# A two-layer audio tower on one core: step 0's state sum through TensorE and ScalarE, and a later load of M3

## What is computed

```python
h = tok(x, W1, b1, W2, b2)                              # patches of 16, two layers
h = h + attn(layernorm(h), w_q, w_k, w_v, w_o)          # quantised, 16 heads
h = h + expert(layernorm(h), w_gate, w_expert, b)       # top-1 of 8, capacity 100
h = h + ssm(layernorm(h), phazor...)                    # a complex decay along the sequence, real part
h = h + moe(layernorm(h), Wg, W1, W2, W3)               # top-2 of 8 experts, 256 -> 512 -> 256
```

## Time and profile before

| what | value |
| --- | --- |
| median of 3 runs | 494.39 us (494.08 to 496.92) |
| profiled execution | 493.69 us, span of its instructions 492.0 us |
| mean granted TensorE clock | 0.951 |
| TensorE matmul busy | 424.3 us (86%) |
| TensorE weight load busy | 263.0 us (53%) |
| VectorE busy | 288.3 us (59%) |
| ScalarE busy | 200.4 us (41%) |
| GpSimd busy | 170.5 us (35%) |
| DRAM traffic | 76 GB/s over the span |

### The profile page before, as it was taken

One profiled execution on the slowest core, in us unless ns is written; L12 is line 12 of the kernel. 1 busy time (PEld: TensorE's weight loads), 2 busy tenths in 40 slices (PEclk: granted clock), 3 DMA queues, 4 the chain that ended last, 5 costly groups with the idle time before them and its releaser, 6 DMA issues.

```text
span 492.0 us, 9443 instructions
## 1 busy us (share of the span) xinstructions
PE 424.3 (86%) x3489; PEld 263.0 (53%) x3490; DVE 288.3 (59%) x885; ACT 200.4 (41%) x373; POOL 170.5 (35%) x141
## 2 busy tenths in 40 slices
PE   0889999995887874878989999999999999999991
PEld 0645456453564653745656766666654444456651
DVE  0498779686688999999996488527751111111110
ACT  1224744662577433325534653255322232333330
POOL 6042010110010115642154536453254565556322
PEclk9999999998887976899899999999999999999996
DMA  9999410046037100563012422152132222322221
GB/s 166 254 202 200 88 48 4 14 156 220 8 94 291 31 20 1 175 223 117 11 45 48 102 39 48 24 137 45 19 57 33 44 37 44 47 45 43 45 23 21
DMA packets 35468, 40.22 MB, mean 82 GB/s; under 512 B 5216, under 2 KB 30048, under 8 KB 35296
## 3 DMA queue, kind: packets, MB, share of 16 engines
q1 hardware_dynamic: 26192, 29.91, 23.0%
q0 software_dynamic: 7040, 9.44, 12.0%
q10 hardware_dynamic: 2192, 0.27, 0.6%
HBM read 28.47 MB, written 8.91 MB: 76 GB/s over the span
## 4 chain that ended last, share of the span: by engine, by line
PE 56%; DVE 18%; DMA 10%; issue 6%; ACT 5%; SPq 3%; POOLq 0%; POOL 0%; DVEq 0%; ACTq 0%
PE psum L2371 21%; PE psum L2392 11%; PE psum L1967 9%; DMA M3s<-in_x_dram 4%; PE psum L1981 3%; DMA out_dram<-O,dst_i 3%; PE psum L2381 3%; DMA out_dram<-O,dst_high 2%; PE psum L1993 2%; PE psum L2353 1%; DVE st_att L1063 1%; SPq L340 1%; DVE H L1313 1%; PE psum L2011 1%; DVE Eb L1105 1%
## 5 line engine op out<-in xcount | busy, mean ns | idle before, releaser
L1860 DVE TENSOR_TENSOR QT<-QT,psum 128x512 f32<-128x512 f32 x36 | 24.7, 687 | 116.0 <-PE psum L2371 113.9
L2371 PE MATMUL psum<-M1s,KT 128*128 (+2 forms) x176 | 68.9, 601 | 2.0 <-issue 1.5
L2392 PE MATMUL psum<-M3s,KT 128*128 (+1 forms) x352 | 69.3, 383 | 1.3 <-ACT KT L855 0.8
L2371 PE MATMUL psum<-M2s,KT 128*128 (+2 forms) x176 | 67.7, 592 | 0.0
L2392 PEld LDWEIGHTS psum<-M3s,KT 128*128 128x128 f32 (+1 forms) x352 | 50.2, 170 | 24.5 <-issue 16.6
L1967 PE MATMUL psum<-M2s,M1s 128*128 128x512 f32 x128 | 58.9, 604 | 0.7 <-ACT H L720 0.7
L866 ACT ACTIVATE O<-psum,gate_slot 128x256 f32<-128x256 f32 x36 | 17.1, 475 | 100.3 <-PE psum L2392 97.4
L522 POOL DMA_INDIRECT KT<-mixture_rows_in,src_i x36 | 40.6, 1127 | 32.3 <-issue 18.0
L2371 PEld LDWEIGHTS psum<-M2s,KT 128*128 128x128 f32 (+1 forms) x176 | 26.0, 171 | 35.8 <-issue 35.8
L549 POOL DMA_INDIRECT out_dram<-O,src_i x17 | 31.4, 1849 | 33.9 <-ACT O L866 14.1
L851 ACT ACTIVATE QT<-psum 128x512 f32<-128x512 f32 x36 | 21.5, 597 | 40.2 <-PE psum L2371 40.2
(11 more groups left out here) (444 smaller groups left out, 786.6 us busy)
## 6 DMA issues: line engine op xcount, KB each, us to landing
M3s<-in_x_dram SPq DMA_DIRECT2D x4, 1024.0 KB, 13.5
M3s<-in_L_ffn_W_dram SPq DMA_DIRECT2D x1, 4096.0 KB, 15.7
M2s<-in_L_ffn_W_dram SPq DMA_DIRECT2D x1, 4096.0 KB, 15.3
M1s<-in_L_ffn_W_dram SPq DMA_DIRECT2D x1, 4096.0 KB, 14.5
M3s<-in_x_dram SPq DMA_DIRECT2D x4, 992.0 KB, 16.8
M1s<-vtok SPq DMA_DIRECT2D x64, 34.0 KB, 1.9
out_dram<-H SPq DMA_DIRECT2D x4, 512.0 KB, 4.1
M1s<-in_L_tok_W_dram SPq DMA_DIRECT2D x2, 512.0 KB, 14.6
```

The lines of the kernel that those rows point to most:

```text
L1860: v.tensor_tensor(sil[:, u, :], sil[:, u, :], bank[3], ALU.mult).then_inc(v_gated, 1)
L2371: last = mm(z[rows, :], xrT[:, u, c, rows], w[:, e, c, :].rearrange("p a h -> p (a h)"), start=(c == 0), stop=(c == CH - 1))
L2392: last = mm(bank[6][rows, 0:DM], actT[:, u, c, rows], M3s[:, e, c, :].rearrange("p a d -> p (a d)"), start=(c == 0), stop=(c == HC - 1))
```

## The change

TensorE no longer only turns step 0's state rows. `state_added` puts H into PSUM first, by a matmul of each H tile with the identity, and accumulates the turned state rows onto it, again by matmuls with the identity. VectorE takes step 0's statistics from PSUM and no longer writes H; it then gives `v_ssm_added` and asks GpSimd by a second small instruction. ScalarE copies the sum from PSUM to H (`ssm_rows`, signal `a_ssm_rows`) and goes on. The rows of H to the output (step 0) and `state_rows(1)`, which uses the same banks, wait for that copy. For steps 1 to 3 the sum stays as it was.

`NORM2_ACT` becomes 1, so ScalarE also writes step 1's normalised rows after the attention. M3's load moves from behind step 1's V transfers to behind step 3's.

```diff
-        NORM2_ACT = 2
+        NORM2_ACT = 1
@@ SP
-                if i == 1:
+                if i == 2:
+                    sp.wait_ge(p_layer1, CH * STEPS)
+                    sp.dma_start(M2s[:], M2.rearrange("e (c p) h -> p e c h", p=P)).then_inc(d_moe, 16)
+                if i == 3:
                     sp.wait_ge(a_sorted, STEPS - 1)
                     sp.wait_ge(v_plane, (STRIDE - RH) * STEPS)
                     sp.dma_start(M3s[:], M3.rearrange("e (c p) d -> p e c d", p=P)).then_inc(d_m3, 16)
-                if i == 2:
-                    sp.wait_ge(p_layer1, CH * STEPS)
-                    sp.dma_start(M2s[:], M2.rearrange("e (c p) h -> p e c h", p=P)).then_inc(d_moe, 16)
...
-                sp.wait_ge(v_ssm_added, i + 1)
+                if i < 1:
+                    sp.wait_ge(a_ssm_rows, i + 1)
+                else:
+                    sp.wait_ge(v_ssm_added, i + 1)
@@ ScalarE
+            def ssm_rows(i):
+
+                act.wait_ge(v_ssm_added, i + 1)
+                a.activation(H[:, TS * i:TS * (i + 1), :].rearrange("p t d -> p (t d)"), banks(4), ACT.Copy
+                             ).then_inc(a_ssm_rows, 1)
+
+            ssm_rows(0)
             gate_exp(2)
             act.wait_ge(v_probsT, BT * STEPS)
+            act.wait_ge(a_ssm_rows, 1)
             norm(SR, 0, X4[0], v_norm4_in, a_norm4)
@@ VectorE
                 dve.wait_ge(p_ssm_rows, i + 1)
+                if i < 1:
+                    norm_stats(S, lambda t_: bank[4 + t_ // 2][:, DM * (t_ % 2):DM * (t_ % 2 + 1)])
+                    v.tensor_scalar(S["ve"][:], S["mv"][:, :, 1], EPS, None, ALU.add).then_inc(v_ssm_added, 1)
+                    dve.wait_ge(v_ssm_added, i + 1)
+                    ask(v.tensor_scalar(S["ve"][:], S["ve"][:], 1.0, None, ALU.mult))
+                    return
@@ TensorE
+            def state_added(i, z):
+
+                def rows(t):
+                    return z[t // 2][:, DM * (t % 2):DM * (t % 2 + 1)]
+
+                for k in range(2):
+                    for t in (k, k + 2):
+                        mm(rows(t), ident[:], H[:, TS * i + t, :], start=True, stop=False)
+                    if k == 0:
+                        pe.wait_ge(v_ssm_out, i + 1)
+                    for t in (k, k + 2):
+                        for c in range(CH):
+                            last = mm(rows(t)[:, P * c:P * (c + 1)], uR[i % 2][:, SN * c + P * t:SN * c + P * (t + 1)],
+                                      ident[:], start=False, stop=(c == CH - 1))
+                last.then_inc(p_ssm_rows, 1)
...
             pe.wait_ge(v_att_rows, STEPS)
-            state_rows(0, bank[4:6])
+            pe.wait_ge(v_ffn_added, 1)
+            state_added(0, bank[4:6])
...
-            pe.wait_ge(v_ssm_added, 1)
+            pe.wait_ge(a_ssm_rows, 1)
             state_rows(1, bank[4:6])
```

More of the change, by code:

```diff
@@ L298, in audio_tower_kernel @@
             sem(n) for n in "a_slot_out a_embed a_expert a_k_masked a_part".split())
-        a_sorted, v_biases, a_plane, v_plane = (
-            sem(n) for n in "a_sorted v_biases a_plane v_plane".split())
+        a_sorted, v_biases, a_plane, v_plane, a_ssm_rows = (
+            sem(n) for n in "a_sorted v_biases a_plane v_plane a_ssm_rows".split())
         block = ctx.enter_context(nc.Block())
```

## The result

| what | before | after |
| --- | --- | --- |
| median | 495.65 us (4 runs, 494.08 to 496.94) | 489.94 us (4 runs, 487.96 to 490.32) |
| profiled execution | 493.69 us, span 492.0 | 489.62 us, span 487.9 |
| mean granted TensorE clock | 0.951 | 0.954 |

The ratio is 0.9878, with a 95% interval from 0.9831 to 0.9925: 1.2% faster, and the interval reaches to within 1% of before. The forecast, 487.6 us against a median of 494.39, was a ratio of 0.9863, with a range of 485.2 to 491.0.

What follows compares the result with a forecast made beforehand. Bound by VectorE from 144 to 251 us and TensorE in the expert slots from 251 to 480, with a TensorE stop in values(1). 3.35 + 2.4 + 0.7 + 0.35 = 6.8 us off 494.39 gave 487.6, range 485.2 to 491.0.

Steps and rivals of the forecast that it cites:

- The stop: TensorE's issue wait in values(1), laid to M3's load delaying an instruction packet: 4.35 us falls to 1.0, gaining 3.35.
- the last term: In values(1), the 1.6 us from the packet's end to TensorE's resumption; if it was load too, no stop is left.
- The clock: Step 3's first three layer-2 tiles, slow after the stop, return to 0.87 us each: 2.4 us gained, other end 0.
- M3's new place: M3's load behind step 3's V transfers costs nothing; other end 2.3 us if the first packet met its traffic.
- NORM2_ACT: Step 1's normalised rows move from VectorE to ScalarE: 0.7 us gained at att_mean(2), ends 0 and 1.2.
- The state sum: Step 0's state sum on TensorE instead of VectorE: 0.35 us gained at state_sum(1), ends -0.3 and 1.1.
- from 207.62 this ends at 211.1: TensorE's matmuls for step 0's state sum take 3.46 us; VectorE wants them at 210.93 and waits 0.2 to 0.3.
- (3): Rival: TensorE runs state_added and what follows at half clock, 7.5 us lost against 6.45 won, 495.4 us; chance 0.02.
- The hold: GpSimd's product holds the port pair shared with VectorE, delaying small operations before state_sum(1); without it 0.55 us gained.
- the likeliest case: The forecast with its own ends, 485.2 to 491.0 us for the whole kernel; chance 0.75.
- (1): Rival: M3's load isn't the cause, the stop in values(1) stays at 4.35 us, time 493.3 us; chance 0.13.
- (2): Rival: the stop moves to step 3's scores under M3's traffic, 492.3 us at worst; chance 0.07.

Runs made afterwards that it cites:

- e4: The changed kernel with 32 instead of 52 warm-up matmuls at TensorE's start; median 487.36 us, ratio 0.9829.
- e9: The changed kernel with three empty instructions on VectorE behind sort_x(0); median 489.26 us, ratio 0.9890.
- e13: e12 with six filler matmuls while TensorE stands idle ahead of the second half of values(3); median 487.47 us, ratio 0.9825.
- e11: e12 with state_added(0) issued ahead of the last three expert tiles of step 2; median 488.63 us, ratio 0.9871.
- e1: The kernel before with only M3's load moved behind step 3's V transfers; median 491.05 us, ratio 0.9892.
- e2: The changed kernel with M3's load put back behind step 1's V transfers; median 494.84 us, ratio 0.9977.
- e5: The kernel before with M3's load at its old place in the queue, but also waiting for the end of step 1's values; median 489.13 us, ratio 0.9885.
- e12: The changed kernel with 32 instead of 52 warm-up matmuls and three empty instructions on VectorE; median 488.36 us, ratio 0.9841.
- e6: The kernel before with 32 instead of 52 warm-up matmuls, M3's load where it was; median 489.74 us, ratio 0.9896.
- e10: e12 with step 0's state sum back on VectorE as in the kernel before; median 487.49 us, ratio 0.9843.

## Why the prediction was right

**The stop.** Right in its mechanism, 0.6 us off in size. I took 1.0 us as what would be left and 1.8 as the end; 1.63 was left, and 1.36 to 1.63 in the six kernels with the load away and nothing shifted. My own terms gave 0.6 + 1.1 + 1.6 - 1.9 = 1.4, and after's are 1.0 + 1.2 + 1.5 - 2.1 = 1.6. So 0.4 of the 0.6 us come from going below that sum in case the last term was load; it wasn't, since 1.3 to 1.5 us from the packet's end to the resumption were there in all six. The start of the packet, which I sized at 0.6 us after the block's entry and which took 1.0 to 1.4, was too small, and the loop (2.10 by the earlier trace rows, not 1.9) makes up for half of it. Gain 2.72 us instead of 3.35.

**The clock.** 2.01 + 1.71 + 1.27 - 1.06 - 0.86 - 0.87 = 2.20 us came back, of 2.4 forecast. The 0.2 between them is no clock: the first tile takes 1.06 us, and not 0.87, in e4 too, which has no stop. A stop of 1.4 to 1.6 us did not lower the clock in any of the six.

**M3's new place.** Right that it costs nothing, though by the slack and not by the packets' good timing: one did meet the traffic (3.9 us), in a stretch with room for it. Step 3's scores and values have no stop. M2's load held a packet back by 4.4 us in before's own trace; I had not counted that block, and it would have spoken for the mechanism.

**NORM2_ACT.** 0.73 us at `att_mean(2)`, forecast 0.7 (0.9 to 1.0 in the other nine kernels that have it). Not foreseen: the 0.46 us idle that the shorter program of VectorE brought with it, of which 0.34 stayed.

**The state sum.** Wrong in sign in the profiled execution: -0.36 us instead of +0.35 (it was +0.5 in e4, e9 and e13). The operations cost about what I priced (3.7 us on TensorE, 1.42 for the statistics from PSUM, 1.03 for ScalarE's copy). The step that failed is "from 207.62 this ends at 211.1": it took the start from before's row, where the eight transposes ahead of it had been at full clock. I had weighed the slow clock as a rival for `state_added` itself (3), and there it did not come; it came one piece of work earlier, where 0.8 us are enough to turn this part. The bound from below (-0.3) was nearly its value. The hold by which a small copy took 0.85 us is there again in e11 (0.66 us, until GpSimd's product ends), as the Trainium skill ("SBUF — State Buffer", two separate sides) has it; but `state_sum(1)` follows 0.14 us behind the product, so the hold costs none of the 0.54.

**The sum.** 2.72 + 2.20 + 0.73 - 0.34 - 0.36, and some 0.24 between the rows, make the 5.19 us by which the slots open earlier. Forecast were 6.8. The median fell by 5.7 us (4.5 against the 494.39 of the forecast, whose fourth run came later), and the time lies inside the range: two terms were too large, one had the wrong sign and one cost was not foreseen, 1.6 us in all, and the likeliest case came about. Of its signs, the stop under 2 us, the tiles at 0.87 and, but for 0.2 us, `state_added` in 3.5 us were met. The transposes came 5.0 us earlier and not 6, and VectorE's 1.26 us before step 0's statistics, where under 0.5 was to show it right, is the state sum's failure. VectorE idle for over 0.5 us before `att_mean(2)` was a bad sign: before had 0.54 already, and after has 0.77.

**The rivals.** (1), that M3's load isn't the cause, falls by e1, e2 and e5, though its weaker half stands: the block comes 1.4 to 1.6 us too late without the load as well. The rule of the Trainium skill ("Runtime: NRT & Kernel Launch", instruction fetch mechanics), that crossing a block's boundary is mostly hidden, holds at the other boundaries that I counted through, `values(0)` in e11 to e13 (below) excepted. It fails where 127 small matmuls with their weight loads run through a block in 2.1 us: 1.63 us quiet, 4.35 with a load. (2), a stop in step 3, did not come. (3) came in a smaller form.

## What to carry to other kernels

A stop with "issue" as its only cause in the middle of a loop of tiny matmuls was a missing block of instructions here: look for the packet, and then either keep large transfers away from it or shift the program (by 40 instructions here), so that the block runs out among large ones. Either gave 1% here, and the kernel that has both, with the change's other two parts (e4), 1.7%. A shift moves all the boundaries behind it, so look at the other loops too: `values(0)` below. And when work moves onto an engine whose clock changes, price the work ahead of it at the slow clock too: the new work's start, not its length, turned this part from a gain into a loss.

## What I had not expected of the hardware

A stop can appear in an earlier loop without any load. In e11, e12 and e13, all with 32 warm-up matmuls, `values(0)` stops for 1.07 to 1.12 us, and in e4, e6 and e10, with the same start of the program, it doesn't. The chain of waits of e12, and the packet in the 0.2 us from 83.2:

```profile
82.58 2.01 PE psum L2030 x118
84.59 1.12 issue
85.71 0.32 PE psum L2030 x5
```

```profile
q8 instruction: 1, 0.02, 33.2%
```

In e4 and e10 there is a packet in the 0.2 us from 78.0 and from 77.2, and the next at 85.2; in e12 none between 72.4 and 83.2. TensorE's work is the same in all of them up to there. So a packet can come 5 us late with nearly no traffic, and I have no cause for it. The same holds for one of before (from 124.4, 3.7 us after its block's entry at 120.9) and one of after (from 126.6, entered at 118.3, with no transfers at all between), which stopped nothing. The reverse stands too: M1's load did not delay the packet at 210.30, and no run here says why.

The clock differs between executions of nearly the same work: `norm2_columns(2)` took 1.09, 1.20, 1.53, 1.64, 1.87, 1.88 and 1.97 us in the profiles. And in e1 two of the first layer-2 tiles, at 35.9 us, ran at the slow level (2.07 and 1.27 us, against 1.13 and 0.86 in after), which put e1's whole profile 1.45 us behind. That, the slots' spread of 1.6 us and the stop in `values(0)` are differences as large as most of those between the medians above, though only the profiled executions show them.
